# Attention and mixture-of-experts block on one core: 512-row pages opened image by image, and images turned inside the expert stage

## The reference

```python
x = x + conv_ref(ln_c(x))      # qkv = W x; q, k l2-normed per head (8 heads of 24); softmax(q k^T * temperature) v; projection
t = to_tokens(x)               # [16, 1024, 192]
n = ln_t(t)
probs = softmax(n @ gate_w + gate_b)              # 4 experts
masked = probs * top2_mask(probs); masked /= masked.sum(-1) + 1e-9
h = gelu(einsum('bsd,edh->ebsh', n, w1) + b1)     # 192 -> 768 in each expert
y = einsum('ebsh,ehd->ebsd', h, w2) + b2
x = from_tokens(t + einsum('bse,ebsd->bsd', masked, y))   # back to [16, 192, 32, 32]
```

## Time and profile before

| | us |
|---|---|
| median of 3 runs | 2742.59 (2740.02 to 2743.46) |
| the profiled execution | 2741.01, its span 2739.1 |
| attention and setup | 0 to about 1694 |
| expert stage | about 1695 to 2660 |
| output stage | from 2663 to the end |

### The profile page before, as it was taken

One profiled execution on the slowest core, in us unless ns is written; L12 is line 12 of the kernel. 1 busy time (PEld: TensorE's weight loads), 2 busy tenths in 40 slices (PEclk: granted clock), 3 DMA queues, 4 the chain that ended last, 5 costly groups with the idle time before them and its releaser, 6 DMA issues. The chain is left out here.

```text
span 2739.1 us, 58873 instructions
## 1 busy us (share of the span) xinstructions
PE 2465.8 (90%) x18693; PEld 1295.9 (47%) x18693; DVE 1683.5 (61%) x4886; ACT 1780.7 (65%) x2228; POOL 1420.5 (52%) x1137
## 2 busy tenths in 40 slices
PE   3699999999989999989999973999999999999975
PEld 2333333333333333333333321777777777777754
DVE  6557766866766766676676655555555555555522
ACT  2487777777778777767777852555565556555542
POOL 2334435534543543543454323677777777777750
PEclk9799999999999999999999987999999999999987
DMA  4221112112112111211211243444444444444429
GB/s 91 58 51 41 50 49 58 48 42 54 51 44 60 48 49 47 58 41 45 59 48 45 77 162 128 179 155 155 177 155 162 169 155 170 160 158 174 153 79 332
DMA packets 160322, 276.49 MB, mean 101 GB/s; under 512 B 21568, under 2 KB 129584, under 8 KB 150624
## 3 DMA queue, kind: packets, MB, share of 16 engines
q1 hardware_dynamic: 141648, 245.37, 27.8%
q0 software_dynamic: 13392, 27.97, 2.8%
q10 hardware_dynamic: 5056, 0.42, 0.3%
HBM read 174.07 MB, written 49.69 MB: 82 GB/s over the span
## 5 line engine op out<-in xcount | busy, mean ns | idle before, releaser
L788 ACT ACTIVATE probs<-ps_s 128x1024 f32<-128x1024 f32 x1024 | 1011.9, 1023 | 282.6 <-PE ps_s L687 260.0
L1360 POOL TENSOR_TENSOR h_split<-h_f,h_split 128x512 f16<-128x512 f32 x444 | 550.7, 1241 | 238.3 <-ACT h_f L1337 231.0
L1333 ACT ACTIVATE h_split<-ps_h,packs 128x512 f16<-128x512 f32 x444 | 305.2, 687 | 391.1 <-PE ps_h L1287 368.8
L1287 PE MATMUL ps_h<-m_xn_t,packs 128*128 128x512 f16 x2220 | 552.4, 380 | 0.5 <-DVE m_xn_t L1422 0.5
L700 PE MATMUL ps_o<-probs,v_aug 128*32 128x512 f32 x4096 | 550.6, 610 | 0.4 <-ACT probs L788 0.4
L1054 POOL TENSOR_TENSOR inv_norm<-sumsq,minus_half 128x16 f32<-128x16 f32 x128 | 378.0, 2953 | 312.4 <-DVE sumsq L997 307.6
L1301 PE MATMUL ps_y<-packs,h_split 128*128 128x192 f16 x5328 | 511.9, 245 | 0.9 <-POOL h_split L1360 0.9
L1301 PEld LDWEIGHTS ps_y<-packs,h_split 128*128 128x128 f16 x5328 | 453.0, 97 | 105.7 <-POOL h_split L1360 1.9
L687 PE MATMUL ps_s<-stacks_odd 98*128 98x512 f16 x1024 | 301.5, 386 | 17.0 <-DMA stacks_odd<-heads 10.2
L687 PE MATMUL ps_s<-even 98*128 98x512 f16 x1024 | 299.0, 383 | 11.6 <-ACT probs L788 5.7
L1337 ACT ACTIVATE h_f<-ps_h,packs 128x512 f32<-128x512 f32 x444 | 302.0, 680 | 0.0
(11 more groups left out here) (213 smaller groups left out, 2812.6 us busy)
## 6 DMA issues: line engine op xcount, KB each, us to landing
packs<-expert_pack SPq DMA_DIRECT2D x74, 1635.0 KB, 6.6
even<-heads SPq DMA_DIRECT2D x192, 96.0 KB, 2.4
stacks_odd<-heads SPq DMA_DIRECT2D x192, 96.0 KB, 2.4
tile_rows<-sorted_rows SPq DMA_DIRECT2D x37, 400.0 KB
tokens<-in_x_dram SPq DMA_DIRECT2D x17, 768.0 KB, 5.3
y_in<-y_tokens SPq DMA_DIRECT2D x16, 768.0 KB, 8.9
out_dram<-y_out SPq DMA_DIRECT2D x16, 768.0 KB, 7.1
even<-heads SPq DMA_DIRECT2D x128, 48.0 KB
```

The costliest lines, as they stand in the source:

```text
L788: act.activation(probs[:, u % PRING, :], ps_s[:, u % 2, :, :].rearrange("p f n -> p (f n)"), ACT.Exp).then_inc(s_probs, 1)
L1287: mm = pe.matmul(ps_h[:, n % HBUF, :], w1(par, slot, w, k), xn_t[0:rows_k, par, c, :], start=(i == 0), stop=(i == 4))
L1333: act.activation(h_split[:, n % HSPLIT, 0, :], ps_h[:, n % HBUF, :], ACT.Gelu, bias=bias1(par, slot, k), scale=1.0 / WSCALE)
L1360: pool.tensor_tensor(h_split[:, n % HSPLIT, 1, :], h_f32[:, n % HBUF, :], h_split[:, n % HSPLIT, 0, :], ALU.subtract).then_inc(s_h, 1)
```

## The change

**Pages instead of segments.** `sorted_rows` now consists of pages of 512 rows. Page i is the input of expert tile i. A pair has one open page; when an image fills it, new pages are taken in order of pairs from a running count. Images are therefore complete one after the other: once the tiles up to 2b + 7 have been computed, image b (counted from 0) is complete, while later tiles are still to come. Pages not fully used hold the rows of a model page: SyncE copies the model page over the next two pages in each image (eight pages ahead of the first). The table and job z are gone. Each row carries its two expert numbers, and SyncE reads these from the first row of a page in DRAM.

**Placement in three pieces.** Job r only copies three sums out of PSUM; `row_pages` in unit 20 counts pages, `row_spots` in unit 22 forms the index. VectorE's routing steps per image go from 36 to 59. The scatters move to units 24 to 27 and 29 to 33. In the late schedule the finish of the image begins three units later.

**Images turned in the expert stage.** From tile 10 on, in every second tile, TensorE transposes one complete image of 1024 tokens (`turn_image`, 8 turns of two transposes, in steps 0 to 5, 10 and 11), through the same bank `ps_j`, and VectorE evicts each turn (`take_image`). A turn waits for the eviction of the turn before. SyncE (`move_image`) stores the image turned before, waits for it to land, and loads the next, between the two pack loads of the tile before. 14 of 16 images go this way; the output stage does the last two.

```diff
+PER = NTOK // TROWS
+FIRST = PER + NPAIR
+MODEL = FIRST + PER * (B - 1)
-LATE_POST_UNITS = tuple(22 + i // 2 for i in range(3 * NT))
+LATE_POST_UNITS = tuple(25 + i // 2 for i in range(3 * NT))
-               "place": 18, "put": (19, 21, 22, 23, 25, 26, 27, 30)}
+               "place": 18, "pages": 20, "spots": 22, "put": (24, 25, 26, 27, 29, 30, 31, 33)}
-ROUTE_STEPS = 36
-TABLE_STEPS = 20
+ROUTE_STEPS = 59
+    def clear_pages(sp, img):
+        sp.wait_ge(s_filled, 16 * (img + 2))
+        first, n = (0, FIRST) if isinstance(img, int) and img == -1 else (FIRST + PER * img, PER)
...
+        sp.dma_start(pages_of(mlp.rows[bass.ds(first * TROWS, n * TROWS), :]),
+                     pages_of(mlp.rows[MODEL * TROWS:(MODEL + 1) * TROWS, :]).to_broadcast([P, n, SLOT * ROW])
+                     ).then_inc(s_filled, 16)
         if has_pre(img):
+            clear_pages(sp, img)
@@ job r, VectorE
-            route.now(dve.tensor_tensor(place[:, :], bank[:, 0:NPAIR], pair_base[:, :], ALU.add))
+            route.mark(dve.tensor_copy(place[:, :], bank[:, 0:NPAIR]))
+            dve.tensor_copy(held[:, :], bank[:, NPAIR:3 * NPAIR]).then_inc(s_job_done, 1)
@@ new, VectorE (3 + 6 instructions, then 6 + 6 and the index)
+    def row_pages(dve, number, route):
+        route.mark(dve.scalar_tensor_tensor(full_at[:, :], old, 1.0 * TROWS, shift_old[:, :], ALU.mult, ALU.add))
+        route.now(dve.tensor_tensor(here, here, before, ALU.add))
...
+    def row_spots(dve, number, route):
+        route.mark(dve.tensor_tensor(spot[:, :, :], by_pair(upto), by_tile(place), ALU.add))
+        route.now(dve.tensor_tensor(shift_new[:, :], new_upto[:, :], new, ALU.subtract))
...
+        for half in s_scatter:
+            dve.wait_ge(half, 8 * NT * number)
+        dve.wait_ge(s_filled, 16 * (number + 1))
+        dve.tensor_copy(index[:, :], index_f[:, :]).then_inc(s_index, 1)
@@ expert stage
+OUT_LAG = 10
+TURN_AT = (0, 1, 2, 3, 4, 5, 10, 11)
+DONE_IMAGES = (NTILE - OUT_LAG + 1) // 2
     def load_pack(sp, i, slot):
-        e = sp.value_load(mlp.table[0:1, 1 + slot, i:i + 1], min_val=0, max_val=NE - 1)
+        named = mlp.rows[i * TROWS:i * TROWS + 1, EXPERT + slot:EXPERT + slot + 1].bitcast(I32)
+        e = sp.value_load(named, min_val=0, max_val=NE - 1)
+    def move_image(sp, b):
+        if b:
+            sp.wait_ge(s_t_done, NT * b)
+            sp.dma_start(out_img[b - 1], y_half[:, :, :]).then_inc(s_out, 16)
+            sp.wait_ge(s_out, 16 * b)
+        if b < DONE_IMAGES:
+            sp.wait_ge(s_put, 16 * SLOT * (2 * b + OUT_LAG - 1))
+            sp.dma_start(y_back[:, :, :], y_img[b]).then_inc(s_in, 16)
+    def turn_image(pe, tile, b, t):
+        if t == 0:
+            pe.wait_ge(s_in, 16 * (b + 1))
+        else:
+            pe.wait_ge(s_t_done, NT * b + t)
+        if TURN_AT[t] >= N_AT and has_next(tile):
+            pe.wait_ge(s_job_done, SLOT * (tile + 2))
+        for k in range(2):
+            mm = pe.transpose(ps_j[0:HC, k * P:(k + 1) * P], y_back[:, t, k * HC:(k + 1) * HC], ident[:, :])
+        mm.then_inc(s_t, 1)
+    def take_image(dve, b, t):
+        dve.wait_ge(s_t, NT * b + t + 1)
+        dve.tensor_copy(y_half[:, :, t * P:(t + 1) * P],
+                        ps_j[0:HC, 0:2 * P].rearrange("p (k n) -> p k n", k=2)).then_inc(s_t_done, 1)
@@ SyncE's loop over tiles
                     load_pack(sp, i + 2, slot)
+                    if slot == 0:
+                        images(sp, i)          # i = 9, 11, ...: move_image(sp, (i - 9) // 2)
+            for i in range(NTILE - 2, NTILE + 2):
+                images(sp, i)
@@ output stage: OUT_BUFS 4 -> 2, over the last two images
+    LEFT = B - DONE_IMAGES
-            for b in range(B):
+            for b in range(LEFT):
```

## The result

The changed kernel takes 2922.4 us (median of 4 runs, 2921.14 to 2927.68) against 2742.8 us of the kernel before in the same session: ratio 1.0661, 95% interval 1.0648 to 1.0674. That is 26 us above the forecast of 2896 us and inside its range.

The account below looks back on a forecast made before the run. TensorE, busy 90% of the span, was taken to bound attention and expert stage, transfers the output stage. Terms -57.7 + 28 + 25 + 54 + 39 + 42 + 3.5 + 20 = +153.8 gave 2896 us beside the median; range 2810 to 2950.

Parts of the forecast that it names:

- output stage: End of the kernel: turning removed for 14 of 16 images, two left; gain 57.7 us.
- transposes of the turns: Expert stage, TensorE: 112 pairs of fp32 transposes at 0.25 us each, all on the path, +28 us.
- turn 7: Expert stage, step 11: TensorE waits 1.9 us for VectorE to evict turn 6, in 13 tiles, +25 us.
- image load: Expert stage: image load queued behind pack load and store lands late, TensorE waits 4.5 us for 12 images, +54 us.
- clock in the expert stage: Half of 3.4 us at the lower clock charged after each of 12 image waits, +20 us.
- waits in attention: Attention, 13 images: added VectorE steps +39 us; later scatters, for which job c waits, +42 us.
- clock in attention: Attention: no clock loss charged, since 1.37 us of TensorE idle had left the clock at 1.00.
- last index: Last image: the index is ready 3.5 us later on the path itself, +3.5 us.
- The rival that had this case (+44 us): Clock falls in attention too, 3.4 us at half rate twice in each of 13 images: 2940 us; chance 0.16.
- The image didn't land in time: Rival in the expert stage: image lands in time, chain from pack issue under 9.5 us, 2822 us; chance 0.13.
- Attention absorbed nothing: Rival: attention takes added steps and later scatters without loss for TensorE, minus 81, 2815 us; chance 0.10.
- Rival 3: TensorE not the true bound; waits vanish through three PSUM buffers, only its work counts: 2716 us; chance 0.08.

Follow-up runs that it names:

- both edits: Changed kernel with the image store and load moved ahead of the first pack load and turn 6's eviction ahead of start_acc: 2795.8 us, ratio 1.0226.
- the one without turns: Changed kernel with pages and three-piece placement kept, but all 16 images turned in the output stage: 2831.1 us, ratio 1.0355.
- image waits alone: Changed kernel with VectorE's eviction of turn 6 moved ahead of start_acc and the token cast: 2872.0 us, ratio 1.05.
- late scatters alone: Kernel before, with no step added and its eight scatters per image moved from units 19 to 30 to units 24 to 33: 2799.7 us, ratio 1.025.
- steps alone: Kernel before with 23 small VectorE operations more per image on an unused buffer, 12 of them waited for: 2799.8 us, ratio 1.0248.
- both together make 3.3 us: Kernel before with the 23 added VectorE operations per image and the scatters in the later units: 2825.0 us, ratio 1.0331.
- half of the steps: Kernel before with 6 waited and 5 unwaited VectorE operations added per image, in place of 12 and 11: 2767.3 us, ratio 1.0119.
- turn-7 waits alone: Changed kernel with the image store and load issued right after the tile's row load, ahead of the first pack load: 2847.0 us, ratio 1.0416.
- one run: Changed kernel with both expert-stage moves, jobs a to c ended at unit 57, routing at units 59 to 63 and 2 to 13, scatters 15 to 23: 2732.7 us.
- The last run: The 2732.7 us kernel with pages operations in unit 12, ranks to pairs two units earlier, scatters one unit later: 2743.7 us, ratio 1.0022.

## Why the prediction was right, and where it was not

| term | forecast | measured | from |
|---|---|---|---|
| output stage | -57.7 | -60.1 | 76.0 to 15.9 us |
| transposes of the turns | +28 | +23.8 | expert stage with both edits, less the one without turns |
| turn 7 | +25 | +29.2, and 3.7 behind it | waits, 13 and 12 |
| image load | +54 | +48.5 | waits, 12 |
| clock in the expert stage | +20 | +23 (estimate) | half of 69 less 22 us at 0.50 |
| waits in attention | +81 | about +56 | 4.3 us idle x 13 images |
| clock in attention | 0 | about +51 | 4.0 us busy x 13 images |
| last index | +3.5 | +3.5 | below |

**The expert stage** came out term by term. The measured terms sum to 128.6 us of 135.6. The store took longer than forecast (9.5 against 8.5 us) and the load less (4.3 against 5.0), so the sum held partly by luck. The Trainium skill (DMA: Bandwidth & Descriptors, Anatomy of one DMA) has 2.0 us plus the bytes over 436 GB/s, by estimate 3.8 us for 768 KB; its fit is for transfers that GpSimd issues, and these are SyncE's. The profile's page of the kernel after has a median of 4.2, nearer to that than the one row I had read, a first load of a stage. The turn-7 wait was forecast at 1.9 us and measured 2.2: in one tile of the trace after, 0.60 us pass from the end of the cast (2285.26) to the transpose (2285.86), where 0.45 was to cover eviction and wait and the eviction alone takes 0.42 (47.1 us for 112).

The clock's 20 us there came out near 23 partly by luck. Its 3.4 us at 0.50 for each of 12 image waits stood beside no row. With the image waits alone it was 56 us at 0.50 (78 less 22), 4.7 us for each; the turn-7 waits, which were charged nothing, alone brought 22 us; and both together 47, less than the two.

**The last index.** TensorE's longest wait, for the first tile's rows, is 21.8 us before and 25.3 after: 3.5 us, as forecast. No run separates its cause.

**The step that failed** is the clock in attention. I charged none because 1.37 us idle had left the clock at full speed, but the same text had just lengthened that idle by 3.0 us. The observation was of another wait than the one I forecast. The trace of the kernel after has 3.36 us idle there and then 0.50. The trace of before could have told me: the wait ahead of the slow clock in the earlier trace rows was 2.61 us (1592.04), and in five attention images TensorE waits 2.3 to 3.0 us ahead of a product of L687 with stacks_odd, four times with the clock at 0.50 behind it. One of them:

```profile
970.03 1.04 PE L687 MATMUL ps_s<-stacks_odd 98*128 98x512 f16 x4 [2.32 <-DMA stacks_odd<-heads]
```
```profile
971.00:972.00 1.00, 1.00 (x9) 0.20 (x8) 0.00 (x0) 1.00 (x2) 0.00 (x0) 0.50 0.00 0
```

The waits that I forecast, 1.37 + 3.0 and 3.2 us, were longer than these. The rival that had this case (+44 us) names what happened, on top of waits that were sized too large.

**The second miss hid half of the first.** The single waits were sized fairly: 3.4 us each for the late scatters alone (forecast 3.2), 2.8 at most for the steps alone (forecast 3.0). But TensorE has part of each back later in the image: its idle time grows by only 2.1 us an image for the steps alone and by 2.0 for the scatters alone, 28 and 27 us in 13 images where I had 39 and 42. And the two don't add: both together make 3.3 us. In the changed kernel's own run the waits come to about 56 us against 81, so 25 too much here and 51 too little for the clock: the attention stage is 26 us longer than forecast. That the whole time came within 26 us is luck to that extent.

**The rivals.** The image didn't land in time (13.8 us from pack to image against the 9.5 that decided). Attention absorbed nothing: even half of the steps cost 33.5 us. Rival 3 fell with them: no wait that was forecast vanished, and the kernel is slower by 180 us.

**What stays open.** In the first session the attention stage of the changed kernel took 1806 us up to the first row load, in an execution 5 us above the median; in the four later kernels with the same attention code it took 1787 to 1789. The kernel before differed by 9 us between the sessions as well. An image had 10.5 us at 0.50 in the first and 9.4 later, which is worth less than half of it. No run tells more; it is why some differences to the change are 5 to 10 us larger by medians than by the stage that was edited. In the expert stage 7 us are unattributed. They are busy time of TensorE: the stage has 30.1 us more of it than with both edits (1001.6 against 971.5), of which the clock explains 23. With the turn-7 waits alone 5.5 us are left over in the same way, with the image waits alone nothing, so they go with the turn-7 waits.

## What to carry to other kernels

Once a term of a forecast makes a wait longer, the clock behind it has to be judged at the new length, by every wait of about that length that the trace of before holds; here, in attention, the clock was as dear as the waits. Two delays that end in the same wait don't add: size the later one from the shifted timeline. And small operations are placed by what stands behind them in their engine's queue. Spreading them over full units brought nothing; moving them, and the scatters behind them, ahead of the rush, with jobs a to c ended earlier, brought 63 us in one run. The last run suggests that the same holds for each other queue that they feed, GpSimd's among them.

## What the runs showed of the hardware

The clock went down with waits shorter than I had thought: it fell inside 3.36 us of idle time and stayed at 0.50 for five microseconds after it, it was at 0.50 behind 2.32 us in the kernel before, and turn-7 waits of at most 2.2 us were enough for 22 us more at 0.50 in the expert stage than with no waits (44 against 22 us). With half of the steps a new wait of 1.8 us in each image (the one shown has another of 0.83 us close behind it) came with 2.6 us more at 0.50 an image, though the image's idle time grew only from 7.59 to 8.19 us. Length alone does not decide: four of those twelve waits left the clock at 1.00, and so did one of 2.27 us for stacks_odd in the kernel before. A register load from DRAM ahead of 74 pack loads cost nothing that can be measured (967.17 and 967.37 us). A 768 KB store issued behind a 1635 KB load on the same queue took 8.9 to 9.7 us to land (9.4 to 10.7 with a 400 KB load between them), and the 768 KB load after it 4.2 us.
